# Expert units of 224 token slots in two tiles of 112 rows, in place of 256 in two of 128

## The chip, the cores and the metric

One core of a Trainium2 chip runs the whole program. The metric is the device time of one execution in microseconds, as the median of several runs.

## The reference

The kernel computes one transformer block on 16 sequences of 100 tokens with 512 features: a gated cross-attention (16 heads, causal) and then a mixture of 8 experts, in which every token goes to one expert. All tensors are float32.

```python
x = x + tanh(g_xattn[0]) * xattn(layernorm(x), ctx_512, Wq, Wkv_expand, Wout)
# _L0_ffn_ref, on the layernorm of that:
x = hidden_states.reshape(-1, 512)              # 1600 tokens
route = sigmoid(x @ router_w)                   # 8 experts
max_ind, max_prob = argmax(route, 1), max(route, 1)
for e in range(8):
    h = silu(x @ gate_w[e]) * (x @ up_w[e])     # 512 -> 1024
    out = out + where(max_ind == e, h @ down_w[e], 0.0)   # 1024 -> 512
out = out * max_prob
x = x + tanh(g_ffn[0]) * out
```

With the reference's inputs the routing, worked out on the host from the reference, sends 194, 202, 179, 199, 214, 200, 214 and 198 tokens to the experts 0 to 7.

## The kernel before, in words

The first part (up to about 240 us) does the attention in four chunks of four sequences. It writes the result x1 of each token to the DRAM table x1_rows and its layernorm to x2_rows. It also routes each token and scatters its number into token_table, in which expert e owns slots from e * SLOTS on, filled from the front. Unfilled slots hold a number out of bounds.

The second part goes over units. A unit is one expert with up to CAP = 256 slots of its list: at least one for each of the 8 experts, and one more for each further CAP slots that an expert fills (more_units). A unit's slots lie in TT = 2 tiles of 128 rows, slot p * TT + t being row p of tile t. For a unit the kernel does this:

- POOL (GpSimd) loads the unit's slots from token_table into idx_next (gather_next, L542), then gathers the rows of x2_rows by an indirect DMA for each tile (gather_tokens, L536). Slots out of bounds are skipped by the DMA.
- TensorE turns the rows (turn_tokens, L1401); ACT and DVE write them as a sum of two float32r values, x_hi and x_lo (split_tokens).
- For each of NJ = 4 slices of 256 hidden columns, gate_up(u, j) multiplies the slice's weights as stationary operand with all tokens as moving operand. Every product is three float32r matmuls (hi by hi, lo by hi, hi by lo; L1147 to L1149, the helper three). So it has 2 (gate, up) x 2 halves x 4 depths x 3 = 48 matmuls that move CAP columns each. Four calls make a unit, 32 make eight units.
- step(u, j): ACT takes the silu (L743), DVE multiplies with up (L1100), ACT and DVE split the result into h_hi and h_lo, and both split the next weights (L611, L780), which SP loads in pieces of 512 KB.
- down(u, j) has the hidden values as stationary operand (128 columns of tokens for each tile) and moves 512 columns of the down weights: 2 tiles x 2 halves x 3 = 12 matmuls.
- finish(u): DVE adds the rows to x1g (L1116), POOL scatters them to the output (send_rows, L562).

The order on TensorE is written out by hand:

```python
with pe.Fori(0, more + (E - 1)) as u:
    gate_up(u, 1)
    down(u, 0)
    gate_up(u, 2)
    down(u, 1)
    turn_tokens(u + 1)
    gate_up(u, 3)
    down(u, 2)
    gate_up(u + 1, 0)
    down(u, 3)
```

The order on POOL in a turn of its loop is send_rows(u), gather_next(u + 2), wait_sent(u), gather_now(u + 1), with gather_now the gather of x1 rows for finish. On DVE finish(u) stands behind step(u + 1, 0).

Of the kernel before, what the change touches and what calls it, by code (L numbers as in the profile page):

```python
# [29 lines left out]
P = 128  # L30
# [41 lines left out]
def flamingo_block(nc, x, ctx, g_xattn, g_ffn, Wq, Wkv, Wout, router_w, gate_w, up_w, down_w, out):  # L72
# [13 lines left out]
    CAP = 256  # L86
    TT = CAP // P
# [25 lines left out]
    with st:  # L113
# [101 lines left out]
        slot_of = sb("slot_of", [P, TT, P], F32)  # L215
# [8 lines left out]
        silu_g = qT[:, 2:4, 0:JC * CAP // 2]  # L224
        h_f = qT[:, 0:2, 0:JC * CAP // 2]
# [201 lines left out]
        def _(pool):  # L427
# [27 lines left out]
            nc.gpsimd.iota(slot_of[:], [[1, TT], [TT, P]], base=0, channel_multiplier=0,  # L455
# [76 lines left out]
            nc.gpsimd.dma_start(idx_now[:], token_table[0:CAP, :].rearrange("(p t) o -> p (t o)", p=P)).then_inc(early_loaded, 16)  # L532

            def gather_tokens(u):
                for t in range(TT):
                    nc.gpsimd.indirect_dma_start(xg[:, t, :], None, x2_rows,  # L536
                                                 bass.IndirectOffsetOnAxis(ap=idx_next[:, t:t + 1], axis=0),
                                                 bounds_check=T - 1, oob_is_err=False).then_inc(xg_loaded.sem, 16)

            def gather_next(base, u):  # L540
                pool.wait_ge(g_lo_done.sem, g_lo_done.after(u, 0))
                nc.gpsimd.dma_start(idx_next[:], token_table[bass.ds(base, CAP), :].rearrange("(p t) o -> p (t o)", p=P)  # L542
                                    ).then_inc(idx_next_loaded.sem, 16)
                pool.wait_ge(idx_next_loaded.sem, idx_next_loaded.after(u - 1, 16))
                pool.sem_inc(wait_passed, 1)
                gather_tokens(u)

            def gather_now(base, u):
                nc.gpsimd.dma_start(idx_now[:], token_table[bass.ds(base, CAP), :].rearrange("(p t) o -> p (t o)", p=P)
                                    ).then_inc(idx_now_loaded.sem, 16)  # L550
                pool.wait_ge(idx_now_loaded.sem, idx_now_loaded.after(u, 16))
                pool.sem_inc(wait_passed, 1)
                for t in range(TT):
                    nc.gpsimd.indirect_dma_start(x1g[:, t, :], None, x1_rows,
                                                 bass.IndirectOffsetOnAxis(ap=idx_now[:, t:t + 1], axis=0),
                                                 bounds_check=T - 1, oob_is_err=False).then_inc(x1g_loaded.sem, 16)

            def send_rows(u):
                for t in range(TT):
                    pool.wait_ge(rows_done.sem, rows_done.after(u, t + 1))  # L560
                    pool.sem_inc(wait_passed, 1)
                    nc.gpsimd.indirect_dma_start(of, bass.IndirectOffsetOnAxis(ap=idx_now[:, t:t + 1], axis=0),  # L562
                                                 rows[:, t, :], None, bounds_check=T - 1,
                                                 oob_is_err=False).then_inc(rows_sent.sem, 16)
# [44 lines left out]
        def _(act):  # L609
# [124 lines left out]
            def split_tokens(u):  # L734
                for t in range(TT):
                    act.wait_ge(gT_ready.sem, gT_ready.after(u, t + 1))
                    copy(x_hi[:, :, t * P:(t + 1) * P], xT_b[t][:].rearrange("p (k s) -> p k s", k=KC)
                         ).then_inc(g_hi_done.sem, 1)

            def step(u, j):  # L740
                act.wait_ge(gu_ready.sem, gu_ready.after(u, j + 1))
                act.wait_ge(h_done.sem, h_done.after(u, j))
                nc.scalar.activation(silu_g, gate_b[j % 2][:].rearrange("p (a n) -> p a n", a=2), ACT.Silu  # L743
                                     ).then_inc(silu_done.sem, 1)
                act.wait_ge(h_done.sem, h_done.after(u, j + 1))
                act.wait_ge(dn_done.sem, dn_done.after(u, j - 1))
                copy(h_hi[:, j % 2], h_f).then_inc(h_hi_done.sem, 1)
                split(u, j, 2)
# [25 lines left out]
        def _(dve):  # L774
# [283 lines left out]
            link(nc.vector.tensor_copy(idx_f[:], idx_now[:]))  # L1058
            split(0, 1, 0)
            dve.wait_ge(found, 1)  # L1060
            link(nc.vector.tensor_tensor(idx_f[:], idx_f[:], found_b[:, 0:TT], ALU.add))
            nc.vector.tensor_copy(idx_next[:], idx_f[:]).then_inc(first_known, 1)
# [27 lines left out]
            def split_tokens(u):  # L1090
                for t in range(TT):
                    dve.wait_ge(g_hi_done.sem, g_hi_done.after(u, t + 1))
                    lo_part(x_lo[:, :, t * P:(t + 1) * P], xT_b[t][:].rearrange("p (k s) -> p k s", k=KC),
                            x_hi[:, :, t * P:(t + 1) * P]).then_inc(g_lo_done.sem, 1)

            def step(u, j):
                dve.wait_ge(silu_done.sem, silu_done.after(u, j + 1))
                dve.wait_ge(h_hi_done.sem, h_hi_done.after(u, j))
                dve.wait_ge(h_lo_done.sem, h_lo_done.after(u, j))
                nc.vector.tensor_tensor(h_f, silu_g, up_b[j % 2][:].rearrange("p (a n) -> p a n", a=2), ALU.mult  # L1100
                                        ).then_inc(h_done.sem, 1)
                dve.wait_ge(h_hi_done.sem, h_hi_done.after(u, j + 1))
                lo_part(h_lo[:, j % 2], h_f, h_hi[:, j % 2]).then_inc(h_lo_done.sem, 1)
                split(u, j, 2)

            def finish(u):

                dve.wait_ge(x1g_loaded.sem, x1g_loaded.after(u, 16 * TT))
                dve.wait_ge(unit_sent.sem, unit_sent.after(u, 0))
                for t in range(TT):  # L1110

                    if t < TT - 1:
                        dve.wait_ge(y_done.sem, y_done.after(u, t + 1))
                    else:
                        dve.wait_ge(dn_done.sem, dn_done.after(u, NJ))
                    nc.vector.scalar_tensor_tensor(out=rows[:, t, :], in0=y_b[t][:], scalar=x1g[:, t, H:H + 1],  # L1116
                                                   in1=x1g[:, t, 0:H], op0=ALU.mult, op1=ALU.add).then_inc(rows_done.sem, 1)
# [26 lines left out]
        def _(pe):  # L1144
# [170 lines left out]
            def find(part):  # L1315

                pe.wait_ge(in_unit_done, part.number + 1)
                for i in range(part.first, part.stop):
                    for t in range(TT):
                        ins = nc.tensor.matmul(found_b[:, t:t + 1], in_unit[0:S, i, t, :], tok_less[0:S, i:i + 1],  # L1320
# [75 lines left out]
            def turn_tokens(u):  # L1396
                pe.wait_ge(xg_loaded.sem, xg_loaded.after(u, 16 * TT))
                pe.wait_ge(g_lo_done.sem, g_lo_done.after(u, 0))
                for t in range(TT):
                    for k in range(KC):  # L1400
                        ins = nc.tensor.transpose(xT_b[t][:, k * P:(k + 1) * P], xg[:, t, k * P:(k + 1) * P], ident[:])  # L1401
# [20 lines left out]
            def down(u, j):  # L1422
# [5 lines left out]
                for t in range(TT):  # L1428
                    for k in range(JC):
                        r = slice(t * P, (t + 1) * P)  # L1430
                        ins = three(y_b[t][:], (h_hi[:, s, k, r], h_lo[:, s, k, r]), (dn_hi[:, s, k, :], dn_lo[:, s, k, :]),
# [49 lines left out]
```

## Time and profile before

| what | value |
|---|---|
| median of 3 runs | 594.67 us |
| the runs | 589.15, 594.67, 595.16 us |
| span of the profiled execution | 593.0 us |
| mean granted TensorE clock | 0.952 |
| TensorE busy | 527.9 us |
| matmuls of L1147 to L1149 with 256 moving columns | 3 x 512 |

The span goes from the first to the last instruction. For the profiled execution no time beside its span is given; the median of the runs is 1.7 us longer than that span, for what lies around it. A clock of 1.00 is 2.4 GHz and one of 0.50 is 1.2 GHz. Matmuls are pipelined, so the busy times of single ones overlap, and their rate is read from the distance between starts.

### The profile page before, as it was taken

How to read it: one execution, taken by the hardware profiler on the slowest of the kernel's cores; microseconds unless marked ns; L12 is line 12 of the kernel's file. 1: busy time of each engine (PE TensorE's matmuls, PEld its weight loads, DVE VectorE, ACT ScalarE, POOL GpSimd, SP SyncE). 2: the span in 40 equal slices, each digit the busy share in tenths (PEclk: the TensorE clock that was granted, in tenths of full speed). 3: DMA queues.
4: the chain of work that ended last, by engine and by line, in shares of the span. 5: the costliest groups of instructions: out<-in, count | busy, mean ns of one | idle time of the engine just before them, and what ended most of it. 6: DMA issues, size and time to landing. Idle time of an engine off the chain costs nothing.

```text
span 593.0 us, 11407 instructions
## 1 busy us (share of the span) xinstructions
PE 527.9 (89%) x3724; PEld 446.4 (75%) x3724; DVE 354.3 (60%) x745; ACT 307.5 (52%) x855; POOL 181.1 (31%) x210
## 2 busy tenths in 40 slices
PE   1999999999899999765999899898997997989991
PEld 1966786587658765555899799797997997979981
DVE  3677579557855576873557557475464563755641
ACT  1898659745974795221445535355353443544520
POOL 5544226315631463325311213112124041121111
PEclk9999999999999999955999999999898998999996
DMA  8400121221120310724475656657377366474620
GB/s 208 141 1 2 52 75 58 70 78 48 43 69 14 85 53 21 257 83 99 136 240 176 218 176 213 228 173 222 113 240 249 122 186 225 156 224 134 239 65 27
DMA packets 58910, 77.31 MB, mean 130 GB/s; under 512 B 5398, under 2 KB 40830, under 8 KB 58880
## 3 DMA queue, kind: packets, MB, share of 16 engines
q1 hardware_dynamic: 53728, 66.90, 36.2%
q0 software_dynamic: 5152, 10.03, 5.5%
q8 instruction: 15, 0.25, 0.2%
q14 instruction: 15, 0.12, 0.1%
HBM read 68.81 MB, written 10.86 MB: 134 GB/s over the span
## 4 chain that ended last, share of the span: by engine, by line
PE 51%; DMA 13%; issue 11%; DVE 8%; ACT 7%; POOL 5%; POOLq 2%; DVEq 1%; ACTq 0%; SPq 0%
PE bank L1147 13%; PE bank L1148 13%; PE bank L1149 13%; DMA x<-x_rows,idx_next 7%; DMA idx_next<-token_table 4%; ACT pr L667 3%; POOL pn L507 2%; PE bank L1242 2%; PE bank L1232 2%; PE bank L1401 2%; POOL out_x L562 2%; DMA staging<-in_L_xattn_Wq 2%; PE bank L1281 1%; ACT wq_hi L611 1%; PE bank L1168 1%
## 5 line engine op out<-in xcount | busy, mean ns | idle before, releaser
L1147 PE MATMUL bank<-x_hi,gu_hi 128*128 128x256 f32 x512 | 147.8, 289 | 2.9 <-ACT qT L743 1.5
L1148 PE MATMUL bank<-x_lo,gu_hi 128*128 128x256 f32 x512 | 147.2, 288 | 0.0
L1149 PE MATMUL bank<-x_hi,gu_lo 128*128 128x256 f32 x512 | 146.9, 287 | 0.0
L1147 PEld LDWEIGHTS bank<-x_hi,gu_hi 128*128 128x128 f32 x512 | 100.4, 196 | 4.3 <-DVE x_lo L780 1.8
L1148 PEld LDWEIGHTS bank<-x_lo,gu_hi 128*128 128x128 f32 x512 | 99.8, 195 | 0.8
L1149 PEld LDWEIGHTS bank<-x_hi,gu_lo 128*128 128x128 f32 x512 | 100.1, 196 | 0.0
L667 ACT ACTIVATE pr<-bank,nmx 100x100 f32<-100x100 f32 x256 | 85.6, 376 | 15.5 <-DVE nmx L960 12.1
L780 DVE TENSOR_TENSOR gu_lo<-staging,gu_hi 128x1024 fp32r<-128x1024 f32 x64 | 76.2, 1221 | 10.8 <-ACT gu_hi L611 9.9
L507 POOL TENSOR_TENSOR pn<-pr,inv 100x400 f32<-100x400 f32 x64 | 54.6, 852 | 78.1 <-DVE inv L953 72.9
L611 ACT ACTIVATE gu_hi<-staging 128x1024 fp32r<-128x1024 f32 x64 | 65.5, 1050 | 16.4 <-DMA staging<-in_L_ffn_gate_w 9.2
L562 POOL DMA_INDIRECT out_x<-xn,idx_now x16 | 21.2, 1327 | 145.8 <-DVE xn L1116 143.4
L667 ACT ACTIVATION_READ_ACCUMULATOR pr<-bank,nmx 100x1 f32 x256 | 61.0, 240 | 0.0
L743 ACT ACTIVATE qT<-bank 128x512 f32<-128x512 f32 x32 | 19.2, 599 | 78.1 <-PE bank L1149 78.1
L1232 PE MATMUL bank<-staging,qT 128*100 128x400 f32 x128 | 53.5, 499 | 0.0
L1100 DVE TENSOR_TENSOR qT<-qT,bank 128x512 f32<-128x512 f32 x32 | 21.9, 686 | 49.6 <-ACT qT L743 45.3
L1147 PE MATMUL bank<-wq_hi,wkv_hi 128*128 128x512 f32 x128 | 50.8, 397 | 0.3 <-DVE wq_lo L780 0.3
L1149 PE MATMUL bank<-wq_hi,wkv_lo 128*128 128x512 f32 x128 | 50.4, 393 | 0.0
L1148 PE MATMUL bank<-wq_lo,wkv_hi 128*128 128x512 f32 x128 | 49.9, 390 | 0.0
L960 DVE TENSOR_REDUCE nmx<-bank 100x4 f32<-100x400 f32 x64 | 36.1, 564 | 19.7 <-PE bank L1232 18.9
L611 ACT ACTIVATE x_hi<-bank 128x400 fp32r<-128x400 f32 (+1 forms) x32 | 16.7, 558 | 56.3 <-PE bank L1149 44.1
L780 DVE TENSOR_TENSOR x_lo<-bank,x_hi 128x400 fp32r<-128x400 f32 (+1 forms) x32 | 19.2, 626 | 42.6 <-ACT x_hi L611 42.6
L969 DVE COPY pT<-bank 100x400 f32<-100x400 f32 x64 | 36.3, 567 | 13.4 <-PE bank L1242 12.9
(182 smaller groups left out, 1008.4 us busy)
## 6 DMA issues: line engine op xcount, KB each, us to landing
staging<-in_L_ffn_gate_w SPq DMA_DIRECT2D x32, 512.0 KB, 5.0
staging<-in_L_ffn_up_w SPq DMA_DIRECT2D x32, 512.0 KB, 6.4
staging<-in_L_ffn_down_w SPq DMA_DIRECT2D x32, 512.0 KB
x_rows<-x SPq DMA_DIRECT2D x8, 800.0 KB
xt<-in_x SPq DMA_DIRECT2D x4, 800.0 KB
xr<-in_x SPq DMA_DIRECT2D x16, 200.0 KB
staging<-in_L_xattn_Wq SPq DMA_DIRECT2D x1, 1024.0 KB, 10.6
x<-in_L_xattn_Wout SPq DMA_DIRECT2D x1, 1024.0 KB, 9.3
```

Source lines behind the costliest of these rows:

```text
L507: nc.gpsimd.tensor_tensor(pn[0:S, n % DEEP], pr[0:S, n % 2], inv[0:S, n % DEEP].unsqueeze(2).to_broadcast([S, HP, S]), ALU.mult).then_inc( ...
L562: nc.gpsimd.indirect_dma_start(of, bass.IndirectOffsetOnAxis(ap=idx_now[:, t:t + 1], axis=0), rows[:, t, :], None, bounds_check=T - 1, oob ...
L611: return nc.scalar.activation(dst, src, ACT.Copy)
L667: ins = nc.scalar.activation(pr[0:S, n % 2, h, :], score_b[n % DEEP][0:S, h * S:(h + 1) * S], ACT.Exp, bias=nmx[0:S, n % DEEP, h:h + 1], a ...
L780: return nc.vector.tensor_tensor(dst, src, hi.bitcast(F32), ALU.subtract)
L960: nc.vector.tensor_reduce(nmx[0:S, b], score_b[b][0:S, 0:HP * S].rearrange("p (h s) -> p h s", h=HP), AX.X, ALU.max, negate=True).then_inc ...
L969: nc.vector.tensor_copy(pT[0:S, m % KEEP], turn_b[m % 2][0:S, 0:HP * S].rearrange("p (h s) -> p h s", h=HP)).then_inc(pT_copied.sem, 1)
L1100: nc.vector.tensor_tensor(h_f, silu_g, up_b[j % 2][:].rearrange("p (a n) -> p a n", a=2), ALU.mult).then_inc(h_done.sem, 1)
L1147: nc.tensor.matmul(dst, a[0], b[0], start=first, stop=False)
L1148: nc.tensor.matmul(dst, a[0], b[1], start=False, stop=False)
L1149: return nc.tensor.matmul(dst, a[1], b[0], start=False, stop=last)
L1232: nc.tensor.matmul(score_b[b][0:S, 0:HP * S], qT[:, m, i * S:(i + 1) * S], keys_b[:, m, i].rearrange("p j s -> p (j s)"), start=False, sto ...
```

## The change

CAP becomes 224, and a tile of a unit has TR = 112 rows in place of 128. Every view of a tile is cut to that: the slots loaded, the rows gathered, turned and scattered (112 in place of 128), the moving operand of gate_up (224 columns in place of 256), the PSUM regions of gate and up (448 columns of the bank), silu, product and split of the hidden values (2 x 224 columns in place of 2 x 256), and the stationary operand of down (112 columns in place of 128). The number of matmuls of a unit stays. The tables of slots keep their size (8 x 224 = 7 x 256 = 1792 slots for an expert); the table of extra units has 56 candidates in place of 48.

The diff, without its unchanged lines, the iota of slot_of and gather_now, which change in the same way:

```diff
--- before.py
+++ after.py
@@ -83,8 +83,9 @@
...
-    CAP = 256
-    TT = CAP // P
+    CAP = 224
+    TT = 2
+    TR = CAP // TT
...
@@ -212,7 +213,7 @@
...
-        slot_of = sb("slot_of", [P, TT, P], F32)
+        slot_of = sb("slot_of", [P, TT, TR], F32)
...
@@ -221,8 +222,8 @@
...
-        silu_g = qT[:, 2:4, 0:JC * CAP // 2]
-        h_f = qT[:, 0:2, 0:JC * CAP // 2]
+        silu_g = qT[:, 2:4, 0:CAP]
+        h_f = qT[:, 0:2, 0:CAP]
...
@@ -529,38 +530,38 @@
...
-            nc.gpsimd.dma_start(idx_now[:], token_table[0:CAP, :].rearrange("(p t) o -> p (t o)", p=P)).then_inc(early_loaded, 16)
+            nc.gpsimd.dma_start(idx_now[0:TR], token_table[0:CAP, :].rearrange("(p t) o -> p (t o)", p=TR)).then_inc(early_loaded, 16)
...
-                    nc.gpsimd.indirect_dma_start(xg[:, t, :], None, x2_rows,
-                                                 bass.IndirectOffsetOnAxis(ap=idx_next[:, t:t + 1], axis=0),
+                    nc.gpsimd.indirect_dma_start(xg[0:TR, t, :], None, x2_rows,
+                                                 bass.IndirectOffsetOnAxis(ap=idx_next[0:TR, t:t + 1], axis=0),
...
-                nc.gpsimd.dma_start(idx_next[:], token_table[bass.ds(base, CAP), :].rearrange("(p t) o -> p (t o)", p=P)
+                nc.gpsimd.dma_start(idx_next[0:TR], token_table[bass.ds(base, CAP), :].rearrange("(p t) o -> p (t o)", p=TR)
...
-                    nc.gpsimd.indirect_dma_start(of, bass.IndirectOffsetOnAxis(ap=idx_now[:, t:t + 1], axis=0),
-                                                 rows[:, t, :], None, bounds_check=T - 1,
+                    nc.gpsimd.indirect_dma_start(of, bass.IndirectOffsetOnAxis(ap=idx_now[0:TR, t:t + 1], axis=0),
+                                                 rows[0:TR, t, :], None, bounds_check=T - 1,
...
@@ -734,17 +735,17 @@
...
-                    copy(x_hi[:, :, t * P:(t + 1) * P], xT_b[t][:].rearrange("p (k s) -> p k s", k=KC)
+                    copy(x_hi[:, :, t * TR:(t + 1) * TR], xT_b[t][:, 0:KC * TR].rearrange("p (k s) -> p k s", k=KC)
...
-                nc.scalar.activation(silu_g, gate_b[j % 2][:].rearrange("p (a n) -> p a n", a=2), ACT.Silu
+                nc.scalar.activation(silu_g, gate_b[j % 2][:, 0:JC * CAP].rearrange("p (a n) -> p a n", a=JC), ACT.Silu
...
-                copy(h_hi[:, j % 2], h_f).then_inc(h_hi_done.sem, 1)
+                copy(h_hi[:, j % 2, :, 0:CAP], h_f).then_inc(h_hi_done.sem, 1)
...
@@ -1055,11 +1056,11 @@
...
-            link(nc.vector.tensor_copy(idx_f[:], idx_now[:]))
+            link(nc.vector.tensor_copy(idx_f[0:TR], idx_now[0:TR]))
...
-            link(nc.vector.tensor_tensor(idx_f[:], idx_f[:], found_b[:, 0:TT], ALU.add))
-            nc.vector.tensor_copy(idx_next[:], idx_f[:]).then_inc(first_known, 1)
+            link(nc.vector.tensor_tensor(idx_f[0:TR], idx_f[0:TR], found_b[0:TR, 0:TT], ALU.add))
+            nc.vector.tensor_copy(idx_next[0:TR], idx_f[0:TR]).then_inc(first_known, 1)
...
@@ -1090,17 +1091,17 @@
...
-                    lo_part(x_lo[:, :, t * P:(t + 1) * P], xT_b[t][:].rearrange("p (k s) -> p k s", k=KC),
-                            x_hi[:, :, t * P:(t + 1) * P]).then_inc(g_lo_done.sem, 1)
+                    lo_part(x_lo[:, :, t * TR:(t + 1) * TR], xT_b[t][:, 0:KC * TR].rearrange("p (k s) -> p k s", k=KC),
+                            x_hi[:, :, t * TR:(t + 1) * TR]).then_inc(g_lo_done.sem, 1)
...
-                nc.vector.tensor_tensor(h_f, silu_g, up_b[j % 2][:].rearrange("p (a n) -> p a n", a=2), ALU.mult
+                nc.vector.tensor_tensor(h_f, silu_g, up_b[j % 2][:, 0:JC * CAP].rearrange("p (a n) -> p a n", a=JC), ALU.mult
...
-                lo_part(h_lo[:, j % 2], h_f, h_hi[:, j % 2]).then_inc(h_lo_done.sem, 1)
+                lo_part(h_lo[:, j % 2, :, 0:CAP], h_f, h_hi[:, j % 2, :, 0:CAP]).then_inc(h_lo_done.sem, 1)
...
@@ -1113,8 +1114,8 @@
...
-                    nc.vector.scalar_tensor_tensor(out=rows[:, t, :], in0=y_b[t][:], scalar=x1g[:, t, H:H + 1],
-                                                   in1=x1g[:, t, 0:H], op0=ALU.mult, op1=ALU.add).then_inc(rows_done.sem, 1)
+                    nc.vector.scalar_tensor_tensor(out=rows[0:TR, t, :], in0=y_b[t][0:TR, :], scalar=x1g[0:TR, t, H:H + 1],
+                                                   in1=x1g[0:TR, t, 0:H], op0=ALU.mult, op1=ALU.add).then_inc(rows_done.sem, 1)
...
@@ -1317,7 +1318,7 @@
...
-                        ins = nc.tensor.matmul(found_b[:, t:t + 1], in_unit[0:S, i, t, :], tok_less[0:S, i:i + 1],
+                        ins = nc.tensor.matmul(found_b[0:TR, t:t + 1], in_unit[0:S, i, t, :], tok_less[0:S, i:i + 1],
...
@@ -1398,7 +1399,7 @@
...
-                        ins = nc.tensor.transpose(xT_b[t][:, k * P:(k + 1) * P], xg[:, t, k * P:(k + 1) * P], ident[:])
+                        ins = nc.tensor.transpose(xT_b[t][:, k * TR:(k + 1) * TR], xg[0:TR, t, k * P:(k + 1) * P], ident[0:TR, 0:TR])
...
@@ -1427,8 +1428,8 @@
...
-                        r = slice(t * P, (t + 1) * P)
-                        ins = three(y_b[t][:], (h_hi[:, s, k, r], h_lo[:, s, k, r]), (dn_hi[:, s, k, :], dn_lo[:, s, k, :]),
+                        r = slice(t * TR, (t + 1) * TR)
+                        ins = three(y_b[t][0:TR, :], (h_hi[:, s, k, r], h_lo[:, s, k, r]), (dn_hi[:, s, k, :], dn_lo[:, s, k, :]),
...
```

## Rows read from the trace of the kernel before

**Rows 1.** The page: busy time by engine, TensorE's clock, the chain's shares

```profile
PE 527.9 (89%) x3724; PEld 446.4 (75%) x3724; DVE 354.3 (60%) x745; ACT 307.5 (52%) x855; POOL 181.1 (31%) x210
...
PEclk9999999999999999955999999999898998999996
...
PE 51%; DMA 13%; issue 11%; DVE 8%; ACT 7%; POOL 5%; POOLq 2%; DVEq 1%; ACTq 0%; SPq 0%
```

**Rows 2.** The page: a DMA queue (packets, MB), and the costliest group

```profile
q0 software_dynamic: 5152, 10.03, 5.5%
...
L1147 PE MATMUL bank<-x_hi,gu_hi 128*128 128x256 f32 x512 | 147.8, 289 | 2.9 <-ACT qT L743 1.5
```

**Rows 3.** The chain of waits, 302 to 340 us: start us, us, what

```profile
302.18 0.87 PE bank L1401 x8
...
317.21 0.60 ACT qT L743
...
321.32 0.75 DVE xn L1116
...
326.04 3.97 DMA idx_next<-token_table
...
332.44 6.59 DMA x<-x_rows,idx_next
```

**Rows 4.** Timeline of TensorE, a unit's first transpose: start, us, [idle before <-releaser]

```profile
339.15 1.09 PE L1401 MATMUL bank<-ident,x 128*128 128x128 f32 x8 [2.33 <-DMA x<-x_rows,idx_next]
...
414.01 1.96 PE L1401 MATMUL bank<-ident,x 128*128 128x128 f32 x8 [2.79 <-DMA x<-x_rows,idx_next]
...
454.72 1.96 PE L1401 MATMUL bank<-ident,x 128*128 128x128 f32 x8 [3.14 <-DMA x<-x_rows,idx_next]
...
532.87 1.96 PE L1401 MATMUL bank<-ident,x 128*128 128x128 f32 x8 [2.51 <-DMA x<-x_rows,idx_next]
```

**Rows 5.** Stretches of 6 us after such a wait: TensorE busy, granted clock, DMA share, GB/s

```profile
339.00:345.00 6.00, 5.85 (x50) 1.00 0.88 303
...
414.00:420.00 6.00, 5.99 (x28) 0.50 0.94 325
454.00:460.00 6.00, 5.28 (x34) 0.72 0.94 303
```

**Rows 6.** Timeline of TensorE, first and last matmul of several runs of equal ones

```profile
264.10 1.87 PE L1320 MATMUL bank<-tok_less,pT 100*128 100x1 f32 x8 [1.48 <-DVE pT L1049]
...
399.84 0.40 PE L1147 MATMUL bank<-wq_hi,wkv_hi 128*128 128x512 f32 x1
...
402.38 0.39 PE L1149 MATMUL bank<-wq_hi,wkv_lo 128*128 128x512 f32 x1
402.61 0.28 PE L1147 MATMUL bank<-x_hi,gu_hi 128*128 128x256 f32 x1
...
408.16 0.28 PE L1149 MATMUL bank<-x_hi,gu_lo 128*128 128x256 f32 x1
...
495.53 0.42 PE L1148 MATMUL bank<-x_lo,gu_hi 128*128 128x256 f32 x1
...
498.31 0.42 PE L1149 MATMUL bank<-x_hi,gu_lo 128*128 128x256 f32 x1
```

**Rows 7.** One line's weight loads by tile: duration ns min/median/max

```profile
L1147 PEld LDWEIGHTS bank<-wq_hi,wkv_hi x128: 187/188/190, 290.7 to 579.9; 128*128 128x128 f32 x128
...
L1147 PEld LDWEIGHTS bank<-wo_hi,ao_hi x64: 163/165/169, 53.6 to 245.4; 128*100 128x100 f32 x64
```

**Rows 8.** The page: costliest groups, each count | busy us, mean ns

```profile
L611 ACT ACTIVATE gu_hi<-staging 128x1024 fp32r<-128x1024 f32 x64 | 65.5, 1050 | 16.4 <-DMA staging<-in_L_ffn_gate_w 9.2
...
L743 ACT ACTIVATE qT<-bank 128x512 f32<-128x512 f32 x32 | 19.2, 599 | 78.1 <-PE bank L1149 78.1
L1232 PE MATMUL bank<-staging,qT 128*100 128x400 f32 x128 | 53.5, 499 | 0.0
L1100 DVE TENSOR_TENSOR qT<-qT,bank 128x512 f32<-128x512 f32 x32 | 21.9, 686 | 49.6 <-ACT qT L743 45.3
```

More of the change, by code:

```diff
@@ L454, in _ @@
                            allow_small_or_imprecise_dtypes=True).then_inc(consts, 1)
-            nc.gpsimd.iota(slot_of[:], [[1, TT], [TT, P]], base=0, channel_multiplier=0,
+            nc.gpsimd.iota(slot_of[:], [[1, TT], [TT, TR]], base=0, channel_multiplier=0,
                            allow_small_or_imprecise_dtypes=True).then_inc(consts, 1)
@@ L548, in gather_now @@
             def gather_now(base, u):
-                nc.gpsimd.dma_start(idx_now[:], token_table[bass.ds(base, CAP), :].rearrange("(p t) o -> p (t o)", p=P)
+                nc.gpsimd.dma_start(idx_now[0:TR], token_table[bass.ds(base, CAP), :].rearrange("(p t) o -> p (t o)", p=TR)
                                     ).then_inc(idx_now_loaded.sem, 16)
@@ L553, in gather_now @@
                 for t in range(TT):
-                    nc.gpsimd.indirect_dma_start(x1g[:, t, :], None, x1_rows,
-                                                 bass.IndirectOffsetOnAxis(ap=idx_now[:, t:t + 1], axis=0),
+                    nc.gpsimd.indirect_dma_start(x1g[0:TR, t, :], None, x1_rows,
+                                                 bass.IndirectOffsetOnAxis(ap=idx_now[0:TR, t:t + 1], axis=0),
                                                  bounds_check=T - 1, oob_is_err=False).then_inc(x1g_loaded.sem, 16)
```

## The prediction

> **What bounds the kernel now.** I read the page first. TensorE is busy for 89% of the span, its granted clock is mostly full, and the chain that ended last lies on it for 51%, with DMA second [rows 1]. The gate and up products are the costliest group, 512 instructions on each of three lines; eight units of 64 make that number, so no expert fills a second unit [rows 2]. Then I followed the chain through one turn of the unit loop, because the order on TensorE and the order on POOL form a ring. The reader should see two halves. From the first transpose of a unit at 302.18 to the silu at 317.21 the chain runs on TensorE: turn_tokens, gate_up(u,3), down(u,2), gate_up(u+1,0). Then it leaves: silu, product, the splits, the finishing addition at 321.32, the two scatters, the load of slots (3.97 us), the second gather (6.59 us), and at 339.15 the next transposes [rows 3, 4]. In this second half TensorE does gate_up 1, down 0, gate_up 2, down 1 beside the chain and then stands still for the gather, for 2.33 to 3.14 us, in all of the six turns of which four are shown [rows 4]. One turn takes 36.97 us when the clock stays full.
>
> The last view is the clock. After two of the six waits it stayed full; after four it was granted at 0.50 (1.2 GHz) for a time, 0.50 and 0.72 as means over 6 us, the other two being 0.72 too [rows 5]. A stretch of 6 us at mean clock c loses 6 x (1 - c): 3.0 + 3 x 1.7 = 8.1 us in the four. The turn that began at 414.01 took 40.71 us.
>
> So a shorter gate_up counts only where TensorE is on the chain. These are 3 calls of unit 0 before the first full turn (0, 1 and 2), two in each of the six turns between 302 and 533 (12), and five after 533, where no gather is awaited any more: 20 of 32. The other 12 lie beside the gather chain, and what they save becomes a longer wait at turn_tokens.
>
> **The change part by part.** *Number of units.* The fullest expert has 214 tokens, under 224, so there are still eight units. With one more the price would be a whole turn, 37 us; the counts exclude it.
>
> *Spacing of the gate and up matmuls.* At the full clock 48 of them start from 402.61 to 408.16, so 0.1181 us apart, and 12 with 512 columns from 399.84 to 402.38, so 0.2309 us apart [rows 6]. That is 0.00044 us a column; for 224 columns the line gives 0.1040, a saving of 0.0141 us each. But each matmul also needs 128 columns of weights, and the change does not shorten that. The load takes 188 ns for 128 columns and 165 for 100 [rows 7]: 0.82 ns a column over a fixed part that overlaps, thus 105 ns of a load that the next one can't share. At the low clock the same is seen directly: 8 matmuls that move a single column behind 128 columns of weights take 1.87 us, at most 0.234 each, while 14 with 256 columns start 2.78 / 13 = 0.214 apart [rows 6]. One column moved is no cheaper than 256, so at the low clock the load sets the pace and 224 columns save nothing. At the full clock no row has fewer than 256 moving columns in float32r. The bounds are 0.104 (the moving operand alone) and 0.118 (nothing gained). The nearest row is that of the transposes, which also load 128 columns and follow each other 0.87 / 8 = 0.109 apart [rows 3]; I take 0.109, a saving of 0.0091.
>
> The Trainium skill, "TensorE: Matmul & The Clock Gate", section "LDWEIGHTS (loading the stationary operand)", says that a load costs its columns divided by 1.2, in ns, whatever the depth. That speaks against this change, which cuts moving columns only; it would put the spacing at 0.107 and the gain from it at 880 x 0.0111 = 9.8 us, an estimate from that page. The slope of the load rows agrees with it [rows 7].
>
> Twenty calls hold 960 matmuls. Some 80 of them run at the low clock: 60 in the four stretches (8.1 us lost at 0.096 each is 84, less 24 transposes) and some 20 in unit 0, before 280 us [rows 1]. The sum is 880 x 0.0091 = **8.0 us** gained, and nothing for the 80. Between the bounds it is 0 to 12.4, or 14.5 if the 80 fall from 0.213 to 0.187 too.
>
> *Element-wise work.* ACT takes 1050 ns for 1024 columns and 599 for 512 [rows 8], 0.88 ns a column, so 0.056 us less for 448. The DVE product takes 686 ns [rows 8]; 64 columns of 512 are at most 0.086, I take 0.066. On the chain of a turn lie silu, product and the first split: 0.18 x 6 = 1.1 us. The split of tokens is hidden behind down(u,2), 12 x 0.231 = 2.8 us, against four operations of 0.6 to 0.7 us in two overlapping pairs; uncovered it would cost some 2.2 us a turn, but it gets shorter, not longer. The finishing addition has 512 columns still, on fewer rows: nothing. Unit 0's path, where nothing covers them, has one split pair and the search for its rows with 112 in place of 128 columns of weights: 0.4 us.
>
> *Transposes.* Eight a unit, from 0.109 to about 0.095 at the full clock and by 0.026 at the low one: 0.11 or 0.21 us, for eight units 1.3 us.
>
> *Down.* It moves 512 columns as before at 0.231; its loads of 112 columns are hidden under that before and after. Nothing.
>
> *Gathers and scatters.* The software queue moved 10.03 MB [rows 2]. The 1600 real tokens alone, gathered twice (2048 and 2080 bytes) and scattered once, make 9.9 MB; 2048 slots would make 12.7. So empty slots moved nothing before, and the DMA does the same work after. Nothing, with 0.2 us a turn as bound either way for landing and for POOL's instructions. The weights loaded are the same, and with a DMA share under 1 in rows 5 they have room.
>
> *Waits and clock.* The gather chain is not shorter, and TensorE comes to it earlier by 2 x 48 x 0.0091 = 0.9 us. The six waits grow from 2.3 to 3.1 to some 3.2 to 4.0 us. Waits of 2.79 and 3.14 were followed by the low clock, and so was one of 2.51, while 2.33 was not [rows 4, 5]. I count all six as followed by it: two more at a mean of 2.0 us, **4.0 us** lost.
>
> *Sum.* 8.0 + 1.1 + 0.4 + 1.3 - 4.0 = 6.8 us less. The span goes from 593.0 to 586.2; the median is 1.7 above the span, so 594.67 becomes **587.9 us**, 1.1% faster.
>
> **The rivals.** *A: the moving operand alone sets the pace.* The straight line from 512 to 256 columns speaks for it, the load row against it. 12.4 + 2.1 + 2.8 - 4.0 = 13.3 us: 581.4.
>
> *B: the spacing doesn't move at all,* because load and stream at 256 columns are already tied, as at the low clock. Waits don't grow, the rest saves 2.8 us: 591.9.
>
> *C: the clock takes it all.* Longer waits make every low stretch as long as the one at 414, 3.0 us: 6 x 3.0 - 8.1 = 9.9 lost, against 10.8 gained: 593.8.
>
> *D, on the other side: float32r with fewer than 256 moving columns is slower, not faster.* Each float32r matmul of this trace moves 256 columns or more, so nothing excludes a narrow form with more passes. The full float32 product shows what passes cost: 128 instructions for 64 products take 53.5 us, 0.84 for one with 400 columns [rows 8], 0.47 scaled to 224. If narrow ones fell to that, 1536 x 0.35 = 540 us, so some 1,130 us; at half of that surcharge about 860. It decides from a spacing of 0.121 on, where 960 x 0.003 eats the 2.8 us of the small terms. Against it: the load explains the low-clock rows without any such rule.
>
> *E: the change doesn't do what it says,* a ninth unit. Price 37 us; excluded by the counts.
>
> **How the numbers follow.** Forecast 0.45, A 0.14, B 0.15, C 0.13, D 0.13, E nothing. A change of 1%, about 6 us, is what a measurement of this kernel can tell, with runs from 589 to 595. Faster by over 1% (under 588.7): two thirds of the forecast's own spread, which with 0.107 to 0.111 as spacing runs from 586 to 590, and all of A, 0.44. Within 1%: the rest of it, B and C, 0.43. Slower: D, 0.13. Range 579 to 596: A with its own few us below, C with the same above. D stays outside, 0.13 left out.
>
> **What would show it.** In the profile after, the starts of gate and up matmuls at the full clock should be 0.109 apart and at the low clock still 0.213; the line of moving columns (0.104) would be A, 0.118 B, more D. The wait before turn_tokens should be 3.2 to 4.0 us and the clock low after each. L743 should average some 0.54 us. A turn should take about 36.97 - 0.9 - 0.3 = 35.8 us plus what the clock costs. The count of 3 x 512 matmuls must stay. The prediction fails most easily on the spacing, which no row here shows, and on the clock, whose four low stretches differ by a factor of two.

## The result, and the profile after

The median of four runs went from 594.54 us to 598.10 (596.23 to 601.32). These two medians are 0.6% apart; the ratio on record is 1.014, 95% interval 1.0086 to 1.0193, and like all ratios here it is formed from runs in the faster of the two states that executions of this kernel fall into. Six more runs of the changed kernel beside eleven of the kernel before gave 1.0132 (1.0077 to 1.0186). The change makes the kernel 1.3 to 1.4% slower. The forecast was 587.9 us, 1.1% faster.

The page of the changed kernel: busy time of TensorE, its granted clock in 40 slices, the software queue, and two of the costliest groups.

```profile
PE 522.1 (88%) x3724; PEld 435.3 (73%) x3724; DVE 349.4 (59%) x745; ACT 303.4 (51%) x855; POOL 189.5 (32%) x210
...
PEclk9999999999999999956899999799898998998996
...
q0 software_dynamic: 5152, 10.03, 6.0%
...
L1148 PE MATMUL bank<-x_hi,gu_hi 128*128 128x224 f32 x512 | 147.8, 289 | 3.3 <-issue 2.1
...
L744 ACT ACTIVATE qT<-bank 128x448 f32<-128x448 f32 x32 | 17.5, 547 | 78.3 <-PE bank L1150 68.5
```

The number of matmuls and the bytes of the software queue stand as before [rows 1, 2], and silu takes 547 ns in place of 599 [rows 8]. The timeline of TensorE shows the new spacing (the rows between are 44 equal ones).

```profile
302.91 0.27 PE L1149 MATMUL bank<-x_lo,gu_hi 128*128 128x224 f32 x1
...
308.05 0.28 PE L1150 MATMUL bank<-x_hi,gu_lo 128*128 128x224 f32 x1
...
338.48 0.98 PE L1402 MATMUL bank<-ident,x 112*128 112x112 f32 x8 [2.96 <-DMA x<-x_rows,idx_next]
376.38 1.75 PE L1402 MATMUL bank<-ident,x 112*128 112x112 f32 x8 [4.34 <-DMA x<-x_rows,idx_next]
416.73 1.75 PE L1402 MATMUL bank<-ident,x 112*128 112x112 f32 x8 [4.51 <-DMA x<-x_rows,idx_next]
457.01 1.75 PE L1402 MATMUL bank<-ident,x 112*128 112x112 f32 x8 [4.13 <-DMA x<-x_rows,idx_next]
496.61 1.18 PE L1402 MATMUL bank<-ident,x 112*128 112x112 f32 x8 [3.12 <-DMA x<-x_rows,idx_next]
535.95 1.75 PE L1402 MATMUL bank<-ident,x 112*128 112x112 f32 x8 [4.16 <-DMA x<-x_rows,idx_next]
```

Forty-six gaps from 302.91 to 308.05 make 0.1117 us each, against 0.1181 [rows 6]. The last six rows are the waits before a unit's transposes, 3.87 us in the mean, where those of before had 2.33 to 3.14, 2.70 in the mean [rows 4]. Stretches of 6 us from four of these transposes (span, busy, granted clock, DMA share, GB/s):

```profile
376.50:382.50 6.00, 6.00 (x35) 0.61 0.76 236
416.50:422.50 6.00, 5.77 (x30) 0.53 0.79 251
457.00:463.00 6.00, 5.99 (x29) 0.50 0.85 271
...
536.00:542.00 6.00, 6.00 (x31) 0.53 0.85 268
```

Of the two that are left out, the one from 338.50 had the full clock and the one from 496.50 a mean of 0.72. Before, such stretches had 0.50 once and some 0.72 three times [rows 5]. Added up over all windows of 1 us from the first unit on, as (1 - clock) times TensorE's busy time in the window, the low clock takes 17.7 us after and 11.0 before. Of that 4.9 and 3.2 us fall into unit 0, before 300 us, and 12.7 and 7.8 into the turns. The mean clock was 0.940 against 0.952 in the profiled executions.

Part of the chain of waits of the changed kernel, from the finishing addition to the next transposes (start, us, what):

```profile
320.42 0.75 DVE xn L1117
...
322.13 0.59 POOL out_x L563
...
325.25 0.95 POOL out_x L563
326.20 2.61 DMA idx_next<-token_table
...
329.76 0.41 POOL x L537
...
331.21 7.14 DMA x<-x_rows,idx_next
338.36 0.12 issue
338.48 0.98 PE bank L1402 x8
```

It is the same ring as in [rows 3]. In its six turns it takes 18.97 us from the addition to the transposes in the mean, against 18.21. The part behind the start of the second gather takes 7.41 against 6.90, which is 0.51 of the 0.76. The other 0.25 is the start of the second gather. It comes either some 11 us after the addition or, where the first gather's instruction takes 1.8 to 2.1 us and not 1.0 to 1.6, some 12 us after it; here four of the six turns are of the late kind, in the profile of before one. The first scatter's instruction takes 2.82 us against 1.73, but the load of slots ends 9.6 us after the addition in both kernels, so that lies under something else.

The balance of the span, 595.8 against 593.0: from the first unit's transposes to its last matmul TensorE stands still 7.6 us more (27.3 against 19.7), the low clock costs 6.7 more, and the work itself is 10.2 us shorter. Another 1.2 us lies ahead of the first unit, whose transposes start at 271.07 and not at 272.30; that is no effect of the change, since the kernel before with the swap (below) has 271.17. What the change saves on TensorE is there. It comes back as waiting and as low clock.

### The profile page after: what moved, and what is told of

It is laid out like the page before. It is cut to its first block, busy times and chain, and to the rows that moved or that the text cites. A ratio compares the mean times of both kernels' runs of the same rounds, so it can differ in the third digit from the quotient of the medians.

```text
span 595.8 us, 11407 instructions
## 1 busy us (share of the span) xinstructions
PE 522.1 (88%) x3724; PEld 435.3 (73%) x3724; DVE 349.4 (59%) x745; ACT 303.4 (51%) x855; POOL 189.5 (32%) x210
## 3 DMA queue, kind: packets, MB, share of 16 engines
q0 software_dynamic: 5152, 10.03, 6.0%
## 4 chain that ended last, share of the span: by engine, by line
PE 45%; DMA 14%; issue 13%; DVE 11%; ACT 7%; POOL 6%; POOLq 2%; DVEq 1%; ACTq 0%; SPq 0%
PE bank L1148 11%; PE bank L1149 11%; PE bank L1150 11%; DMA x<-x_rows,idx_next 7%; DMA idx_next<-token_table 3%; ACT pr L668 3%; DMA xt<-in_x 3%; POOL pn L508 2%; PE bank L1243 2%; PE bank L1233 2%; POOL out_x L563 2%; PE bank L1402 2%; DVE norm_bn L829 1%; PE bank L1282 1%; ACT wq_hi L612 1%
## 5 line engine op out<-in xcount | busy, mean ns | idle before, releaser
L1148 PE MATMUL bank<-x_hi,gu_hi 128*128 128x224 f32 x512 | 147.8, 289 | 3.3 <-issue 2.1
L1149 PE MATMUL bank<-x_lo,gu_hi 128*128 128x224 f32 x512 | 147.0, 287 | 0.0
L1150 PE MATMUL bank<-x_hi,gu_lo 128*128 128x224 f32 x512 | 145.2, 284 | 0.0
L563 POOL DMA_INDIRECT out_x<-xn,idx_now x16 | 28.3, 1771 | 146.5 <-DVE xn L1117 144.1
L744 ACT ACTIVATE qT<-bank 128x448 f32<-128x448 f32 x32 | 17.5, 547 | 78.3 <-PE bank L1150 68.5
L1149 PE MATMUL bank<-wq_lo,wkv_hi 128*112 128x512 f32 x128 | 50.7, 396 | 0.0
L1148 PE MATMUL bank<-wq_hi,wkv_hi 128*112 128x512 f32 x128 | 50.5, 394 | 0.2 <-DVE wq_lo L781 0.2
L1150 PE MATMUL bank<-wq_hi,wkv_lo 128*112 128x512 f32 x128 | 50.5, 395 | 0.0
L1101 DVE TENSOR_TENSOR qT<-qT,bank 128x448 f32<-128x448 f32 x32 | 19.8, 618 | 49.6 <-ACT qT L744 49.6
L781 DVE TENSOR_TENSOR wq_lo<-staging,wq_hi 128x1024 fp32r<-128x1024 f32 x32 | 39.2, 1225 | 10.4 <-ACT wq_hi L612 10.4
```

The source lines that it names most:

```text
L744: nc.scalar.activation(silu_g, gate_b[j % 2][:, 0:JC * CAP].rearrange("p (a n) -> p a n", a=JC), ACT.Silu).then_inc(silu_done.sem, 1)
L781: return nc.vector.tensor_tensor(dst, src, hi.bitcast(F32), ALU.subtract)
L1101: nc.vector.tensor_tensor(h_f, silu_g, up_b[j % 2][:, 0:JC * CAP].rearrange("p (a n) -> p a n", a=JC), ALU.mult).then_inc(h_done.sem, 1)
L1148: nc.tensor.matmul(dst, a[0], b[0], start=first, stop=False)
L1149: nc.tensor.matmul(dst, a[0], b[1], start=False, stop=False)
L1150: return nc.tensor.matmul(dst, a[1], b[0], start=False, stop=last)
```

## The experiments

Times are medians of the runs; ratios are to the kernel before, on the same chip. Two experiments can lie on different chips, so they are best compared by their ratios. Chain, landing and waits come from one profiled execution each. "Chain" is the mean, over the six turns of the profiled execution, from the finishing addition to the next transposes; "landing" its part from the start of the second gather; "lost" the sum of (1 - clock) x busy as above, unit 0 included.

**The changed kernel again.**

> The changed kernel once more, beside the kernel before on the same chip, as the yardstick for the parts. In the first measurement it took 598.1 us and the part with 224 columns alone 592.5. If the loss of 1% is the kernel's own, it is 596 to 600 us again, ratio 1.007 to 1.014; if it came from the chip or from the few runs, 591 to 594 us, ratio within 0.3% of 1.

598.64 us, 1.0132. The loss repeats: chain 18.66, landing 7.66, lost 17.4, of which 3.2 in unit 0. Here the second gather starts late in one turn only, so it is the later landing that repeats, and not the late start.

**Fewer columns alone.** The kernel before, its gate and up products moving 2 x 112 of the 256 columns; no gather or scatter changes. Slots from 112 on in each tile hold no token.

```diff
-ins = three(bank[:, m * CAP:(m + 1) * CAP], (gu_hi..., gu_lo...), (x_hi[:, k, 0:CAP], x_lo[:, k, 0:CAP]), ...)
+ins = three(halves(bank[:, m * CAP:(m + 1) * CAP]), (gu_hi..., gu_lo...), (halves(x_hi[:, k, 0:CAP]), halves(x_lo[:, k, 0:CAP])), ...)
```

> The kernel before, with one part of the change: gate_up moves 224 columns (two runs of 112 of each tile's 128), everything else is as before; the columns left out belong to empty slots. Theory R (the ring: what TensorE saves beside the gather chain becomes waiting, and longer waits bring more low clock): matmuls start 0.112 apart, the first scatter of a turn on POOL stays at 1.74 us, the waits before the transposes grow from 2.7 to some 3.4 us on average, and the time is 588 to 594 us (ratio 0.99 to 1.00). Rival P (the loss is the spacing of narrow matmuls itself, or the clock reacting to them): the time is near that of the whole change, 598 us, ratio 1.01.

592.54 us, 0.9996 (0.9967 to 1.0025). The spacing fell to 0.111, landing stayed 6.87, the mean wait grew to 3.42 and the clock fell to 0.944 (0.956 in the runs of before beside it). So the columns bring nothing while the ring stands, and cost nothing either: the 1.3% needs another part. The low clock in the turns took 13.4 us against 7.8 in the profile of before. These 5.6 us more are as much as 880 narrower matmuls save (880 x 0.0064 = 5.6).

**Rows of the scatter, both ways.** The changed kernel scatters 128 rows (the index tile and the rows are filled once at the start), and the kernel before scatters 112.

```diff
-nc.gpsimd.indirect_dma_start(of, bass.IndirectOffsetOnAxis(ap=idx_now[0:TR, t:t + 1], axis=0), rows[0:TR, t, :], ...)
+nc.gpsimd.indirect_dma_start(of, bass.IndirectOffsetOnAxis(ap=idx_now[:, t:t + 1], axis=0), rows[:, t, :], ...)
```

> The changed kernel, with the two scatters of a unit over 128 rows of idx_now again (rows 112 to 127 hold numbers out of bounds, so nothing more is sent). Theory S (a scatter of 112 rows falls differently against DVE's splits and holds POOL 1.07 us longer in each turn): the first scatter of a turn takes 1.74 us again and not 2.81, the chain from the finishing addition to the next transposes gets about 1 us shorter, the waits fall from 3.9 to about 3 us, and the time falls by 6 to 12 us to 587 to 592. Rival (the 1.07 us comes from when the work falls, not from the rows): still 2.8 us and 596 to 599 us.

> The kernel before, with the two scatters of a unit over 112 rows in place of 128 and nothing else changed (slots from 224 on are empty in every unit, so the output is the same). Theory S: the first scatter of a turn takes 2.8 us in place of 1.74, the waits before the transposes grow by about 1 us to 3.7 us on average, more of them are followed by the low clock, and the time rises by 6 to 12 us to 601 to 606 (ratio 1.01 to 1.02). Rival: the scatter stays at 1.74 us and the time at 594.

The first gave 592.84 us, 1.0014 (0.9976 to 1.0051), the second 590.28, 0.9945 (0.991 to 0.998). The timelines of POOL, first scatter after the addition, of the changed kernel with 128 rows and of the kernel before with 112:

```profile
320.51 2.88 POOL L565 DMA_INDIRECT out_x<-xn,idx_now  x1 [21.29 <-DVE xn L1119]
```

```profile
322.70 1.67 POOL L562 DMA_INDIRECT out_x<-xn,idx_now  x1 [22.15 <-DVE xn L1116]
```

The scatter of 128 rows is still long in the changed kernel, the one of 112 short in the old one. Its length is not set by its rows, and the theory that this long instruction is the loss fell. The rival was right on the instruction and wrong on the times: it had 596 to 599 us for the first run and 594 for the second. The long instruction runs beside DVE's pair of gu_lo splits in both kernels, and what lengthens it was not tried by itself. The Trainium skill, "SBUF — State Buffer", section "SBUF: two separate sides", says that VectorE with two operands in SBUF and GpSimd (when its operation reads SBUF) share ports which one of them holds for a whole instruction; no run here shows that by itself.

The first of the two runs matters for the whole argument. It still gathers over 112 rows, its landing is still 7.42 us, and yet the loss of 1.3% is gone. In its profile the second gather starts early in all six turns, 10.81 us after the addition, which brings the chain to 18.23 (18.21 before) and the mean wait to 3.13. Whether the rows of the scatter do that, and why, no run shows. In the kernel before 112 rows made it 0.5% faster although its chain was longer (18.59), with 6.5 us lost to the clock. So the time of this ring can move by 1% through a part whose mechanism stays open here.

**The ring taken out.** On POOL the rows of unit u+2 are gathered before those of unit u are sent, in both kernels.

```diff
-send_rows(u)
 gather_next(first_slot(u + 2), u + 2)
+send_rows(u)
```

> The kernel before, with gather_next(u + 2) ahead of send_rows(u) in POOL's loop, so that the slots and rows of the next unit are fetched while TensorE still works on the unit, and no longer behind its finishing addition. Theory R (the ring of finish, scatter, load of slots and gather bounds six turns): the waits of 2.3 to 3.1 us before the transposes vanish, with them the low clock after them, and the kernel gets faster by 16 us of waits and some 8 us of low clock, to 566 to 574 us, ratio 0.96. Rival (the weights' DMA or the splits on ACT and DVE are as late as the gather): 585 us or more, and new waits at L1147 for the split of weights.

> The same swap in the changed kernel. Theory R: with no ring every one of the 1536 narrower matmuls counts, 0.0064 us each = 9.8 us, and with the shorter transposes and splits it is 9 to 12 us faster than the kernel before with the swap: 556 to 563 us. Rival (the change costs something of its own beside the ring, on POOL, in the gathers or in the clock): no more than 3 us under the kernel before with the swap.

570.56 us (0.9659, 0.9614 to 0.9705) for the kernel before with the swap and 561.02 (0.949, 0.9445 to 0.9535) for the changed one. The changed one's page:

```profile
PEclk9999999999999999995599999999999999999997
```

its timeline at the transposes:

```profile
333.36 0.93 PE L1402 MATMUL bank<-ident,x 112*128 112x112 f32 x8
366.70 0.93 PE L1402 MATMUL bank<-ident,x 112*128 112x112 f32 x8
400.02 0.93 PE L1402 MATMUL bank<-ident,x 112*128 112x112 f32 x8
```

and the same rows of the kernel before with the swap:

```profile
337.13 1.03 PE L1401 MATMUL bank<-ident,x 128*128 128x128 f32 x8
371.73 1.04 PE L1401 MATMUL bank<-ident,x 128*128 128x128 f32 x8
406.34 1.03 PE L1401 MATMUL bank<-ident,x 128*128 128x128 f32 x8
```

No row has a wait, and after unit 0 the clock stays full in both. A turn takes 33.33 us in place of 34.61; 192 matmuls at 0.0064 less make 1.23 of that. The change as a whole is worth 9.5 us (1.7%) once TensorE is on the chain for every call. This is the fastest version, 5.1% under the kernel before.

**The clock held.** Sixteen matmuls of 400 columns, whose result nobody reads, are put before the wait for the gathered rows, in both kernels.

```diff
+pe.wait_ge(g_lo_done.sem, g_lo_done.after(u, 0))
+for f in range(16):
+    nc.tensor.matmul(xT_b[1][:, 0:CT], x_hi[:, 0, 0:P], x_hi[:, 1, :], start=True, stop=True)
 pe.wait_ge(xg_loaded.sem, xg_loaded.after(u, 16 * TT))
```

> The changed kernel with 16 idle matmuls of 400 columns (2.9 us at the full clock) on TensorE ahead of the wait for the gathered rows; turn_tokens overwrites what they write. They shorten no wait of the ring and only keep TensorE busy in most of it. Theory C (most of what the change lost is low clock after the longer waits): the clock stays at 1.00 in the turns, the kernel loses some 13 us of low clock and takes 584 to 588 us. Rival (the loss sits in the chain itself): 595 us or more.

> The same 16 matmuls in the kernel before. Theory C: it had less low clock to lose (4 to 8 us), so it takes 585 to 589 us, and the gap of 1.3% between the changed kernel and this one closes to within 0.4% (in the ring the change saves 0.6 us a turn on TensorE's half and loses about as much in the chain of gathers). Rival: the gap stays at 6 to 8 us.

587.45 us (0.9952, 0.9922 to 0.9982) for the changed kernel and 591.06 (1.0002, 0.9973 to 1.003) for the one before. The changed kernel's page:

```profile
PEclk9999999999999999955899999999999999999997
```

and two of its stretches behind the transposes:

```profile
378.50:384.50 6.00, 6.00 (x55) 1.00 0.96 312
453.50:459.50 6.00, 6.00 (x55) 1.00 0.91 294
```

The low clock is left in unit 0 only (lost 3.4 in the one, 3.3 in the other). In the changed kernel the chain is 18.70 and five of six transposes still wait for the gather, so the ring still sets the turns. In the kernel before it does not:

```profile
374.80 3.05 PE L1400 MATMUL bank<-x_hi 128*128 128x400 f32 x16
377.69 1.03 PE L1404 MATMUL bank<-ident,x 128*128 128x128 f32 x8
```

Here and in four more of the six turns the transposes follow the 16 matmuls without a wait: these take 2.89 us, longer than the gather needs. Such a turn takes 37.50 us, where the two of full clock in the profile of before take 37.14 and 37.24, so by an estimate from these rows the idle matmuls themselves cost this kernel some 2 us in six turns. With the clock held the change is 3.6 us faster, of which up to these 2 us may be theirs; without, it is 4 to 8 us slower (3.6 in the first comparison, 7.8 in the repeat). They save the changed kernel 11 us, as Theory C had it, and the kernel before next to nothing, where it had expected 585 to 589 us and a gap within 0.4%; the gap turned round, to 0.6%. That the low clock carries most of the loss of the changed kernel is shown; how much of the gap it makes is shown only roughly.

**What sets the spacing.** The changed kernel with the swap, gate and up products moving 160 of 224 columns (the tokens in the other slots get no hidden values).

> The changed kernel with the swap, with gate_up moving only 160 columns (80 of each tile's 112; tokens in the slots from 160 on get no hidden values). Theory L (a load of 128 columns of weights sets the pace below some 240 moving columns): the spacing stays at 0.110 to 0.112 us, and the time at 559 to 562 us. Rival (the moving columns still set it, by the line 0.0047 + 0.00044 a column): 0.075 us apart, and some 50 us less. A narrow form with more passes would show more than 0.112.

```profile
298.27 0.28 PE L1149 MATMUL bank<-x_lo,gu_hi 128*128 128x160 f32 x1
...
302.30 0.28 PE L1149 MATMUL bank<-x_lo,gu_hi 128*128 128x160 f32 x1
```

Thirty-six gaps make 0.1119 us each, the turns are 33.29 us against 33.33. So with 128 columns of weights the spacing has a floor of 0.112, whether 224 or 160 columns move. The time of its two runs, 565.69 us (0.9575), lies above the 559 to 562 expected and above that of 224 columns. The difference of the two profiled spans, 6.1 us, stands ahead of the turns: the second unit's transposes start at 306.33 and not at 300.04, after a longer low clock in unit 0 (lost 11.9 us there against 3.4).

**Rows of the gather.** The changed kernel gathers x2 over 128 indices again, the empty ones filled once; then the kernel before gathers over 112.

```diff
-nc.gpsimd.indirect_dma_start(xg[0:TR, t, :], None, x2_rows, bass.IndirectOffsetOnAxis(ap=idx_next[0:TR, t:t + 1], axis=0), ...)
+nc.gpsimd.indirect_dma_start(xg[:, t, :], None, x2_rows, bass.IndirectOffsetOnAxis(ap=idx_next[:, t:t + 1], axis=0), ...)
```

> The changed kernel with the gathers of x2 rows over 128 rows of idx_next again (rows 112 to 127 out of bounds, nothing more moves). Theory G (the 112-row gather lands later: 7.4 to 7.7 us from its start to the transposes, against 6.9 before): it is 6.9 again and the time falls by 4 to 6 us to 592 to 595. Rival (it lands later because the weights' loads start earlier against it): still 7.4 us and 596 to 600 us.

> The kernel before, with the gathers of x2 rows over 112 rows in place of 128 and nothing else changed (rows from 112 on hold no tokens). Theory G (a gather of 112 rows lands some 0.5 us later by itself): from the second gather's start to the transposes 7.4 us in place of 6.9, waits longer by 0.5 us, more low clock, 594 to 597 us, ratio 1.004 to 1.009. Rival (it takes the earlier times of the changed kernel as well): 6.9 us still, and a ratio within 0.3% of 1.

The changed kernel with 128 rows: 593.50 us, 1.0046 (1.0021 to 1.007), some 5 us back; landing 6.86, chain 18.08, wait 2.99. The kernel before with 112 rows: 598.65, 1.010 (1.0062 to 1.0138), landing 7.47, chain 18.77, wait 3.27, a little more than the 594 to 597 expected (its profile is of one of its longest executions, 603.20 us). Time from the gathers' issue to landing (min, median, max), of the changed kernel, and of it with 128 rows:

```profile
DMA to landing us min/median/max: 3.3/7.0/7.6
```

```profile
DMA to landing us min/median/max: 3.3/6.4/7.2
```

The same of the kernel before, and of it with 112 rows:

```profile
DMA to landing us min/median/max: 3.3/6.1/7.3
```

```profile
DMA to landing us min/median/max: 3.2/6.9/8.0
```

Both directions agree: the shorter list of indices, with the same tokens in it, lands later by 0.5 us in the turns of the ring.

**The two parts together.** 224 columns and gathers over 112 rows in the kernel before, nothing else.

> The kernel before with two parts of the change alone: gate_up moves 224 columns and the gathers of x2 rows go over 112 rows. If these two are the whole loss, it takes 596 to 600 us like the changed kernel, ratio 1.009 to 1.014, with a mean granted clock of 0.94 and waits of some 3.9 us. Rival (a third part, such as the scatters or the narrower element-wise work, is needed): 592 to 594 us.

597.84 us, 1.0122 (1.0085 to 1.0159); wait 4.15, landing 7.42, clock 0.939. Two of the change's parts are enough for the whole loss (1.0132, 1.014). They are not all that decides it: the changed kernel with scatters over 128 rows has both of them and stands at 1.0014, and the one with gathers over 128 rows keeps 0.5% of the loss.

**Other numbers of rows.** The kernel before with gathers over 120 and over 108 rows.

> The kernel before, with the gathers of x2 rows over 120 rows in place of 128. Theory N (the later landing grows with the rows taken away from the end, as if the transfers of the remaining ones were shared out differently over the DMA engines): between the two, 7.1 to 7.2 us from the second gather to the transposes, ratio 1.003 to 1.006. Rival T (128 is special, any smaller number pays in full): 7.4 us, ratio 1.01. Rival Z (112 is special): 6.9 us, ratio within 0.3% of 1.

> The same with 108 rows. Theory N: 7.5 us or more and a ratio of 1.01 to 1.013. Rival T: 7.4 us and 1.01, as with 112. Rival Z: 6.9 us and within 0.3% of 1.

606.71 us, 1.0303 (1.0254 to 1.0353), and 606.12, 1.0262 (1.0209 to 1.0315). The same view of the gathers with 120 rows, then with 108:

```profile
L536 POOL DMA_INDIRECT x<-x_rows,idx_next x16: 1092/1106/1895, 267.5 to 535.2; - x16
...
DMA to landing us min/median/max: 3.5/6.6/8.1
```

```profile
L536 POOL DMA_INDIRECT x<-x_rows,idx_next x16: 1086/1098/2159, 266.4 to 539.6; - x16
...
DMA to landing us min/median/max: 3.5/6.5/8.0
```

The chain took 19.18 and 19.12 us and its landing part 7.98 and 7.36. The 7.36 is a mean of two kinds of turn. In three of the six the second gather started some 1.1 us late and then landed in 6.49 to 6.90; in the other three the landing part is 7.98, as with 120 rows. By such turns with an early start it is 7.00 for 128 rows, 7.55 for 112 and 7.98 for 120 and for 108. All the theories written down ahead of these two runs fell: the cost does not follow the number of rows (128, 120, 112, 108 give 0, 3.0, 1.0 and 2.6%). The two numbers that 16 does not divide are the dear ones, and in both the shortest gather instruction took 1.09 us where it is 1.00 to 1.02 with 128 or 112 rows; that is an observation on four sizes, no mechanism. Nor does the software queue's work explain it: it moved 10.03 MB each time, in 5152 packets with 128, 120 and 112 rows and in 5408 with 108. Why 112 rows land later than 128 is open.

## Why the prediction was wrong, step by step

*The ring, and which calls count.* The ring is right. Without it the turn's saving is that of all four calls. With it the run with 224 columns alone shows the whole saving turned into longer waits and low clock; that just 20 of 32 calls count was not tested by itself. The full-clock turn was read as 36.97 us from the chain, which misses the first part of the transposes; from start to start of the transposes it is 37.14 (302.01 to 339.15). The same turn of the changed kernel takes 36.46, so 0.7 us less where 1.2 were forecast.

*The spacing.* The mechanism was right, the size was off: a floor by the weight load, at 0.1117 and not 0.109, so 880 x 0.0064 = 5.6 us in place of 8.0. The Trainium skill, "TensorE: Matmul & The Clock Gate", section "LDWEIGHTS (loading the stationary operand)", would give 0.107; the measured 0.1117 decides, 5% above. That 160 columns go no faster shows that the load holds the floor. At the low clock the spacing stayed 0.214, as forecast (16 gaps from 418.48 to 421.90). Rivals A, B and D are out.

*Number of units, element-wise work, transposes.* Right: 3 x 512 matmuls, 547 ns (forecast 0.54), transposes 0.93 us in place of 1.03 for eight. The 10.2 us of shorter work stand against 1536 x 0.0064 = 9.8 and 1.3 for the transposes.

*"Gathers and scatters ... Nothing, with 0.2 us a turn as bound."* This step failed. The bytes are the same, as it said, but bytes were not what was to be priced: these gathers are the last part of the chain in each turn, and in these runs their latency depends on the length of the index list. Over 112 rows they land 0.5 us later, 3 us in six turns before any effect on the clock, and the run with this part alone costs 1.0%. That the scatters could matter was excluded by the same words, and they move the time by 0.5 to 1.2%, in a way that stays open. The bound of 0.2 us had no row under it.

*The waits.* Right in size, 3.2 to 4.0 forecast and 3.87 in the mean measured (2.96 to 4.51), but the reason given covers only half of it, so the size came out by luck. TensorE comes 6 x 96 x 0.0064 = 3.7 us earlier by its narrower matmuls. The chain behind the addition is 6 x 0.76 = 4.6 us longer, 3.1 of it landing and 1.5 the later start of the second gather. Ahead of the addition it is some 1 us shorter (317.21 to 321.32 before, 316.48 to 320.42 after, so 0.17 in this turn). That makes 7.3; the six waits grew by 7.0.

*The clock.* All six waits were counted as followed by the low clock at a mean of 2.0 us, 4.0 us more. Five of the six were, and the turns lost some 5 us more; another 1.7 us came in unit 0, where profiles of one kernel differ as much (4.9 and 3.2 in the two of the changed kernel). Together it was 6.7 more. Rival C (9.9 lost of 10.8) was nearest in mechanism, but it, too, left out the gathers. Part of the miss is the profile of before: its clock of 0.952 is low for that kernel, whose runs beside the experiments had 0.956 to 0.959 in the mean, while the changed kernel's ten had 0.935 to 0.945, 0.940 in the mean. That fits the 3.6 us between the first medians and 7.8 in the repeat.

*The sum with measured terms:* 5.6 + 1.1 + 0.4 + 1.3 saved, 4.6 lost in the chain of gathers and 6.7 to the clock, 2.9 us slower by the span, against 2.8 measured. So close a match is in part luck, since spans of one kernel differ by several us.

That the sign hangs on the ring, the gather latency and the clock is shown by the pairs: with the ring out the change is 9.5 us faster, with the clock held 3.6 faster (less what the idle matmuls cost the kernel before), and with 128-row gathers the loss shrinks from 1.3 to 0.5%. Two things stay open: why 112 rows land later, and why scatters over 128 rows take the loss away as well.

## What to carry to other kernels

Before an edit to the tile's size is priced by its work, follow the chain of waits to the transfer at its end, and treat the length of that transfer's index list as a term of its own, even where the bytes stay the same. Work removed from an engine that waits in a ring comes back as a longer wait, and here on TensorE as a lower clock: first take out the ring (here one swap of two calls on POOL, 3.4%), then the same edit pays (1.7% more).

## What the runs showed of the hardware

Float32r matmuls behind 128 columns of weights start 0.1181 us apart with 256 moving columns and 0.1117 to 0.1119 with 224 and with 160. An indirect gather of the same some hundred rows of 2 KB takes a time that depends on the length of its index list, though it does not simply rise or fall with it. In the turns of the ring in which the second gather starts early, its landing part is 7.00 us for 128, 7.55 for 112 and 7.98 for 120 and for 108, and the whole kernel takes 1.010, 1.0303 and 1.0262 of the time with 112, 120 and 108. Sixteen idle matmuls of 400 columns in a wait of 3 to 4.5 us kept the clock at 1.00 behind it, in each of the turns. Without them the mean over the 6 us behind such a wait was 0.50 to 0.72 in five of six turns.
